# Row maxima of attention scores from a difference: positive part on ScalarE, sum and maximum on VectorE, scores in three PSUM banks

## The reference

```
q, k = _rope(q), _rope(k)
sim = jnp.einsum('bhid,bhjd->bhij', q, k) * SCALE
attn = jax.nn.softmax(sim, axis=-1)
out = jnp.einsum('bhij,bhjd->bhid', attn, v)
out = out.transpose(0, 2, 1, 3).reshape(b, n, HEADS * DIM_HEAD)
return out @ Wout + bout
```

## Time and profile before

| | us |
|---|---|
| median of 3 runs (1556.73 to 1557.29) | 1557.01 |
| time of the profiled execution | 1557.27 |
| its span, first to last instruction | 1555.5 |
| PE / PEld busy | 1424.9 / 546.8 |
| DVE busy, of it the 512 reductions L603 | 1222.0, 623.9 |
| ACT busy, of it the 1024 exps L515 | 778.3, 547.8 |
| POOL busy, of it the sums L676 | 977.8, 616.5 |
| PE idle ahead of unit matmuls (L397) until DVE's maximum was done | 47.7 |

### The profile page before, as it was taken

One profiled execution on the slowest core, in us unless ns is written; L12 is line 12 of the kernel. 1 busy time (PEld: TensorE's weight loads), 2 busy tenths in 40 slices (PEclk: granted clock), 3 DMA queues, 4 the chain that ended last, 5 costly groups with the idle time before them and its releaser, 6 DMA issues.

```text
span 1555.5 us, 25971 instructions
## 1 busy us (share of the span) xinstructions
PE 1424.9 (92%) x7289; PEld 546.8 (35%) x7289; DVE 1222.0 (79%) x1297; ACT 778.3 (50%) x1512; POOL 977.8 (63%) x501
## 2 busy tenths in 40 slices
PE   3689999999999999999999999999999999998886
PEld 1224333333333333333333333333333333333323
DVE  7787888788788878878788888878887887888744
ACT  3244554545454545555455454545545554544464
POOL 4388766658475665838476574848566584757731
PEclk9799999999999999999999999999999999999999
DMA  5312131221303121120313122031312204031002
GB/s 158 73 26 60 25 76 26 50 54 26 83 14 75 34 57 38 44 65 14 75 34 74 22 54 54 14 79 30 75 21 54 54 20 89 14 75 33 3 15 68
DMA packets 70209, 76.00 MB, mean 49 GB/s; under 512 B 27204, under 2 KB 36936, under 8 KB 69928
## 3 DMA queue, kind: packets, MB, share of 16 engines
q1 hardware_dynamic: 68736, 74.69, 21.4%
q10 hardware_dynamic: 1448, 1.00, 0.3%
HBM read 22.56 MB, written 2.36 MB: 16 GB/s over the span
## 4 chain that ended last, share of the span: by engine, by line
PE 56%; DVE 13%; issue 13%; POOL 7%; DMA 5%; ACT 3%; SPq 2%; DVEq 0%; ACTq 0%; POOLq 0%
PE O L388 18%; PE S L376 10%; PE S L377 8%; PE M L397 8%; DVE MX L603 5%; PE TILE L312 5%; DVE SUM L613 4%; DMA QK<-STAGE 4%; POOL SA L676 3%; PE TILE L322 2%; POOL STAGE L663 2%; ACT PF L515 2%; SPq L708 1%; PE TILE L306 1%; PE TILE L330 1%
## 5 line engine op out<-in xcount | busy, mean ns | idle before, releaser
L676 POOL TENSOR_TENSOR SA<-PF 128x1024 f32<-128x1024 f32 x256 | 616.5, 2424 | 372.5 <-DVE SUM L610 279.9
L515 ACT ACTIVATE PF<-S 128x512 f32<-128x512 f32 x1024 | 547.8, 599 | 564.9 <-PE S L377 564.1
L603 DVE TENSOR_REDUCE MX<-M 128x1 f32<-128x1024 f32 x504 | 614.5, 1219 | 229.3 <-PE M L397 229.1
L388 PE MATMUL O<-PF,V 128*64 128x512 f32 x2048 | 497.4, 607 | 0.0
L376 PE MATMUL S<-QK 128*128 128x512 f16 x1024 | 393.1, 384 | 0.0
L377 PE MATMUL S<-QK 128*128 128x512 f16 x1024 | 390.1, 381 | 0.0
L397 PE MATMUL M<-QK 64*128 64x512 f16 x1008 | 221.9, 437 | 65.9 <-DVE MX L603 47.7
L613 DVE TENSOR_TENSOR SUM<-SUM,SA 128x1024 f32<-128x1024 f32 x128 | 248.3, 1939 | 3.6 <-POOL SA L676 3.4
L397 PEld LDWEIGHTS M<-QK 64*128 64x128 f16 x1008 | 72.6, 140 | 370.8 <-DVE MX L603 247.9
L388 PEld LDWEIGHTS O<-PF,V 128*64 128x64 f32 x2048 | 124.5, 136 | 206.4 <-issue 149.8
L376 PEld LDWEIGHTS S<-QK 128*128 128x128 f16 x1024 | 99.9, 98 | 165.3 <-issue 64.2
(11 more groups left out here) (96 smaller groups left out, 749.0 us busy)
## 6 DMA issues: line engine op xcount, KB each, us to landing
QK<-STAGE SPq DMA_DIRECT2D x128, 256.0 KB, 3.9
QK<-STAGE SPq DMA_DIRECT2D x128, 128.0 KB, 3.1
RB<-den SPq DMA_DIRECT2D x128, 128.0 KB, 3.0
X<-in_L_attn_queries SPq DMA_DIRECT2D x4, 512.0 KB, 12.8
RT<-DS SPq DMA_DIRECT2D x128, 2.0 KB, 1.7
out<-X SPq DMA_DIRECT2D x8, 256.0 KB, 2.3
WRAW<-in_L_attn_Wkv SPq DMA_DIRECT2D x1, 1024.0 KB, 8.7
ROPE<-in_rope SPq DMA_DIRECT2D x1, 1024.0 KB, 12.0
```

The source lines that it names most:

```text
L388: mm = e.matmul(O[DH * z:DH * z + DH, :], V[:, h, kt * DH:(kt + 1) * DH], PF[:, t % SLOTS, z * HALF:(z + 1) * HALF], start=(kt == 0), stop ...
L515: e.activation(PF[:, t % SLOTS, z * HALF:(z + 1) * HALF], S[:, t % 2, z * HALF:(z + 1) * HALF], ACT.Exp, scale=EXP_SCALE).then_inc(exped, 1)
L603: e.tensor_reduce(MX[:, place % 2, q:q + 1], bank, AX, ALU.max).then_inc(max_read, 1)
L676: e.tensor_tensor(SA[:, (t // 2) % 2, :], PF[:, t % SLOTS, :], PF[:, t % SLOTS + 1, :], ALU.add).then_inc(two_summed, 1)
```

## The change

Of a query row a unit now gives, in place of 1024 products, two times 512: its products with the differences of keys k and k+512 (in the new bank MD), and those with keys 512 and up (in one of two new banks MR). Since max(a, b) = b + max(a - b, 0), ScalarE writes the positive part of MD to LEFT in SBUF (`act_left`, Relu), and VectorE adds LEFT and MR and takes the maximum of the row in one `tensor_tensor_reduce`. POOL makes the differences of the high parts of the keys once per group (`pool_keys_less`), and `hand_over` copies them too, with six DMAs per head instead of four. K is projected before Q, and several tiles change their steps. The scores get three banks in turn, MD one, MR two, O and T one each. A score matmul waits for the exp that last read its bank. ACT's copy of O stands behind the exps of its step and no longer ahead of them. Three small weight buffers share space with SA.

```diff
-HAND = 4 * 16
+LOWEST = -3.0e38
+HAND = 6 * 16
-QK_TILES = [(w, c, t) for w in "qk" for c in range(2) for t in ("rot", "pass")]
+ORDER = "kq"
+QK_TILES = [(w, c, t) for w in ORDER for c in range(2) for t in ("rot", "pass")]
-QK_AT = (1, 3, 5, 7, 9, 11, 13, 15)
-V_AT = {8: (1, 0), 10: (1, 1), 22: (0, 0), 24: (0, 1)}
+QK_AT = (1, 3, 4, 7, 8, 10, 11, 13)
+KD_AT = 9
+V_AT = {14: (1, 0), 16: (1, 1), 22: (0, 0), 24: (0, 1)}
-NORM_AT = {16: 1, 26: 0}
+NORM_AT = {13: 1, 26: 0}
-DOWN_AT = (12, 14, 16, 18, 21, 23)
+DOWN_AT = (12, 18, 21, 22, 23, 24)
...
-        S = pb("S", [P, 2, N], F32)
-        M = pb("M", [P, N], F32)
+        S = pb("S", [P, 3, HALF], F32)
+        MD = pb("MD", [P, 512], F32)
+        MR = [pb(f"MR{n}", [P, 512], F32) for n in range(2)]
...
+        def bank_of(t, z):
+
+            return ((0, 1), (2, 0))[t % 2][z]
...
-                wait(e, exped, 2 * n + z - 3)
+                wait(e, exped, 2 * n - ((0, 2), (3, 1))[t % 2][z])
...
+        def pe_unit(e, u, place, q, side):
+
+            wait(e, left_over, u)
+            wait(e, max_read, u - 1)
+            e.matmul(MD[:, :], QHH[0:DH, place, q:N:KT], KD[:, place, :], start=True, stop=True)
+            e.matmul(MR[side][:, :], QHH[DH:P, place, q:N:KT], KMH[DH:P, place, 512:N],
+                     start=True, stop=True).then_inc(unit_made, 1)
...
+        def act_left(e, u, side):
+
+            e.wait_ge(unit_made, u + 1)
+            wait(e, max_read, u - 1)
+            e.activation(LEFT[:, side, :], MD[:, :], ACT.Relu).then_inc(left_over, 1)
...
-            if kt == 2 and (not it.first or h > 0):
-                act_copy_out(e, it.i * GH + h - 1, (h - 1) % GH)
+            more = not (it.last and t + LEAD >= STEPS)
+            if t % 2 == 0 and more:
+                act_left(e, it.step(t + LEAD), t % 2)
             for z in range(2):
...
+            if kt == 2 and (not it.first or h > 0):
+                act_copy_out(e, it.i * GH + h - 1, (h - 1) % GH)
             act_tiles(e, it, t)
+            if t % 2 == 1 and more:
+                act_left(e, it.step(t + LEAD), t % 2)
...
-            e.wait_ge(unit_made, u + 1)
-            e.tensor_reduce(MX[:, place % 2, q:q + 1], bank, AX, ALU.max).then_inc(max_read, 1)
+            e.wait_ge(left_over, u + 1)
+            e.sem_inc(max_begun, 1)
+            e.tensor_tensor_reduce(LEFT[:, side, :], MR[side][:, :], LEFT[:, side, :], 1.0, LOWEST, ALU.add, ALU.max,
+                                   MX[:, place % 2, q:q + 1]).then_inc(max_read, 1)
...
+        def pool_keys_less(e, g):
+
+            e.wait_ge(rot_hi, g * 4 + 2)
+            e.wait_ge(pass_hi, g * 4 + 2)
+            keys = HIGH["k"]
+            e.tensor_tensor(KDS[:, :, :], keys[:, :, 0:512], keys[:, :, 512:N], ALU.subtract).then_inc(keys_less, 4)
...
                 sp.dma_start(QK[top, h, 0:3:2, :], STAGE[rows, 1:3, t, :]).then_inc(handed[h], 16)
+                sp.dma_start(KD[top, h, :], KDS[rows, t, :]).then_inc(handed[h], 16)
...
             for u in range(LEAD):
-                wait(pe, max_read, u - 2)
-                pe_unit(pe, u, u // KT, u % KT, (M[:, :], S[:, 0, :], S[:, 1, :])[u % 3])
-            pe.wait_ge(max_read, LEAD)
+                pe_unit(pe, u, u // KT, u % KT, u % 2)
```

More of the change, by code:

```diff
@@ L374, in pe_scores @@
                 rows = slice(z * HALF, (z + 1) * HALF)
-                wait(e, exped, 2 * n + z - 3)
-                e.matmul(S[:, t % 2, rows], KHL[:, h, keys], QHH[:, h, rows], start=True, stop=False)
-                e.matmul(S[:, t % 2, rows], KMH[:, h, keys], QML[:, h, rows],
+                wait(e, exped, 2 * n - ((0, 2), (3, 1))[t % 2][z])
+                e.matmul(S[:, bank_of(t, z), :], KHL[:, h, keys], QHH[:, h, rows], start=True, stop=False)
+                e.matmul(S[:, bank_of(t, z), :], KMH[:, h, keys], QML[:, h, rows],
                          start=False, stop=True).then_inc(scored, 1)
@@ L391, in pe_values @@
             mm.then_inc(pv_done, 1)
-        def pe_unit(e, u, place, q, bank):
-            for c in range(2):
-                rows, keys = slice(DH * c, DH * c + DH), slice(c * 512, (c + 1) * 512)
-                mm = e.matmul(bank[:, keys], QHH[rows, place, q:N:KT], (KHL, KMH)[c][rows, place, keys],
-                              start=True, stop=True)
-            mm.then_inc(unit_made, 1)
+        def pe_unit(e, u, place, q, side):
[4 more added lines that the diff above has]
+                     start=True, stop=True).then_inc(unit_made, 1)
         def pe_next_unit(e, it, u):
@@ L405, in pe_next_unit @@
                 e.wait_ge(handed[place], HAND * (it.i + u // STEPS + 1))
-            e.wait_ge(max_read, it.step(u))
-            pe_unit(e, it.step(u), place, q, M[:, :])
+            pe_unit(e, it.step(u), place, q, u % 2)
         def pe_step(e, it, t):
@@ L596, in split_ff_weights, with dve_max @@
                                    ALU.subtract).then_inc(f_w_lo, 1)
[L598 to L600 removed]
+        def dve_max(e, u, head, place, q, side):
             if q == 0:
                 wait(e, max_found, head - 1)
[L603 removed]
+            e.wait_ge(left_over, u + 1)
+            e.sem_inc(max_begun, 1)
+            e.tensor_tensor_reduce(LEFT[:, side, :], MR[side][:, :], LEFT[:, side, :], 1.0, LOWEST, ALU.add, ALU.max,
+                                   MX[:, place % 2, q:q + 1]).then_inc(max_read, 1)
         def dve_sum(e, head, h, part):
@@ L685, in pool_step @@
                     rot_add(e, args, it.i + 1)
+            if t == KD_AT and not it.last:
+                pool_keys_less(e, it.i + 1)
             if t % 2 == 0 and (not it.first or t > 0):
@@ L807, in _ @@
                     rot_low(pool, args, 0)
+                    if args[0] == "k" and args[1] == 1:
+                        pool_keys_less(pool, 0)
             ln_rstd(pool, 1)
@@ L862, in _ @@
             act.wait_ge(b1_turned, 1)
-            act.activation(B1[:, :], M[:, 0:FF // P], ACT.Copy).then_inc(b1_copied, 1)
-            act_max(act, 0, 0)
+            act.activation(B1[:, :], MR[0][:, 0:FF // P], ACT.Copy).then_inc(b1_copied, 1)
+            for u in range(LEAD):
+                act_left(act, u, u % 2)
+                if u == KT + 1:
+                    act_max(act, 0, 0)
             def body(e, it):
```

45 lines of the change are left out of this document (25 added, 20 removed).

## The result

The changed kernel takes 1571.32 us (median of four runs, 1569.38 to 1572.88) against 1556.91 (1556.73 to 1557.29): a ratio of 1.0092, 95% interval 1.0074 to 1.0109. It is slower by 14 us, where the forecast was 20 us faster, and lies above the range. The profiled execution took 1572.87 us with a span of 1570.9.

What follows compares the result with a forecast made beforehand. TensorE (92% busy) sets the pace, late mainly for VectorE's maxima. Loop -14.4, first iterations -4.6 and -2.6, last -2, start +4.2: -19.4, say -20, from about 1557 to 1537 us; range 1528 to 1546.

Steps and rivals of the forecast that it cites:

- rival B: VectorE's fused sum and maximum costs 1.37 us, delaying low parts at steps 4 and 8: 1553 us, chance 0.15.
- D: Rival: VectorE itself binds, if GpSimd slows the fused instruction to 1.85 us per unit: 1610 us, chance 0.05.
- Rival A: Neighbour tiles at steps 10 and 11 cost nothing, so 1.8 us more go in 15 iterations: 1510 us, chance 0.12.
- step 11: Q rot tile, waiting for the bank until VectorE's low part of step 10's tile: 1.8 us, where 0.35 stood.
- Rival C: ScalarE's alternating positive part, exp and copy don't overlap, pitch 0.60 not 0.48 us: 1575 us, chance 0.15.
- Rival E: The change works, but small waits add 1.2 us per iteration more than counted: 1556 us, chance 0.08.
- step 28: PV matmuls wait for ScalarE's copy of O, now behind the exps: 0.7 us per iteration.
- step 4: Tile there waits 0.3 us for the low part of step 3's tile, plus 0.1 for the unit.
- out17: Output tile of step 17, behind the V tile of step 16: a new wait of 0.15 us.
- The loop's sum: Late starts removed against new ScalarE and tile-bank waits: -0.9 us per iteration, -14.4 for sixteen.
- First iterations -4.6 -2.6: Extra gains there: two hand-over waits of 2.9 us, not 0.6 (-4.6); MX waits 8.0, not 2.6 (-2.6).
- Last -2: Last iteration waits a little more than others for maxima, so it gains 2 us extra.

Runs made afterwards that it cites:

- e8: Changed kernel with the twelve units ahead of the loop in more banks: 1567.13 us, ratio 1.0069 to the kernel before.
- e5: Changed kernel with only ScalarE's fourteen middle iterations written out instead of a loop: 1551.10 us, ratio 0.9962 to the kernel before.
- e1: Changed kernel with the Q/K tiles of steps 11 and 13 moved to steps 12 and 15: 1565.46 us, ratio 1.0033 to the kernel before.
- e14: Changed kernel with the high part of a step's tile ahead of ScalarE's copy of O: 1550.18 us, ratio 0.9952 to the kernel before.
- e10: Changed kernel with ScalarE's positive part over 256 of 512 columns in the loop: 1566.91 us, ratio 1.0066 to the kernel before.
- e3: Changed kernel with the fourteen middle iterations written out in every engine: 1543.05 us, ratio 0.9899 to the kernel before.
- e2: Changed kernel with O copied between the two exponentials of its step: 1569.76 us, ratio 1.0066 to the kernel before.
- e15: Changed kernel with the copy of O back ahead of the step's exponentials: 1595.07 us, ratio 1.0240 to the kernel before.
- e4: Kernel before with its fourteen middle iterations written out in every engine: 1560.56 us, ratio 1.0018 to the kernel before.

## Why the prediction was wrong, step by step

The mechanisms of VectorE were right. The three waits for the maximum, the hand-over wait and the normalisation's are gone. The fused operation takes 0.69 + 0.08 us (forecast 0.85, rival B 1.37; B and D fall). Rival A falls by the 1.90 at step 11. Rival C, the one on the slower side, had ScalarE's instructions 0.60 apart and named 0.54 as the limit. A positive part and the exponential behind it do start 0.61 apart in most steps, but there the exponential waits for its scores: it starts 2.97 behind the PV, 0.12 behind the end of its matmul, as the forecast had it. Where it need not wait they are 0.49 apart, with ScalarE written out 0.53, and an exponential and the positive part behind it 0.48. So C is refuted although its time, 1575, came near. Rival E, small waits of 1.2 us an iteration more than counted, is what the quiet iterations show; its time, 1556, lacks the clock and the first and last iterations. First scores 61.19: forecast 61.0, although only 2 us of the delay come from the bank I blamed (e8).

The new waits that I had named were right one by one: step 11 1.90 (1.8), step 28 0.73 (0.7), step 4 0.32 (0.4 with its unit), out17 0.14 (0.15). The groups view of VectorE in the changed kernel:

```profile
L625 DVE CUSTOM_DVE_ANT_0 LEFT<-MR,LEFT 128x512 f32<-128x512 f32 x512 | 353.3, 690 | 481.8 <-ACT LEFT L517 477.1 <-issue 3.4
...
L625 DVE DVE_READ_ACCUMULATOR2_ANT MX<- 128x1 f32 x512 | 42.2, 82 | 0.0
```

What failed, of the 35.4 us between forecast (-20, rounded from -19.4) and profiled spans (+15.4):

- **The loop's sum, "-4.77 + 3.85 = -0.9": 19.4 us in the fourteen middle iterations, the clock's 3.3 among them.** I walked the 32 steps inside an iteration and not across its end. ScalarE's turn of 2.5 us had been hidden by its idle 2.82 us, and I filled that time with a positive part at each side of the turn. It made step 1 0.96 late where I had 0.16: 0.8 of the miss. Missing too were 0.32 at PV of step 4 (same cause as step 28, where I did see it) and 0.16 behind the V tile, while three of the other four bank waits are 0.07 and not 0.16. These make 1.0; a quiet iteration is 1.2 above the forecast, 16 us in fourteen, and 0.2 I can't place. e5 shows that step 1 is on time when ScalarE alone has no loop. The order on ScalarE is not part of this miss: its wait at step 11 was forecast at 1.8.
- **The clock.** Those 3.3 us, and one stretch of half clock more in the last iteration. The first has one of 3.4 us behind step 11, where the kernel before had one of about 7 us behind its hand-over wait. I had priced the wait of 1.8 us at 1.8. In the middle iterations of e1 and e14, where it is gone or shortened, there are no falls.
- **"First iterations -4.6 -2.6": about 6 us.** The earlier trace rows has one long hand-over wait, not two, so 2.3 were never there. The rest: transposes of steps 26 and 27 come 3.04 and 1.84 us late, where one was 1.14 late before, each for the low part of the tile ahead of it (e14 left them as they are), and step 11 with the clock behind it. In VectorE's queue the first of these low parts stands behind a sum that waited 4.78 us for GpSimd (the row below this list). GpSimd works there without a gap for some 46 us in both kernels (from 106.56 after, from 101.88 before). Counted from the first scores, TensorE ends the scores of step 26 5.6 us sooner than before, and GpSimd starts its sum only 0.5 sooner. So much of what the waits for maxima and hand-over gave back was lost again there. This is read from the traces; no run changed it by itself.
- **"Last -2": 7.5 us.** GpSimd works without a gap there for some 36 us from step 7 on, in both kernels, at the normalised rows that TensorE transposes, and so little could be won; a second stretch of half clock (1.7 us), the copy of O, and the tiles moved together came on top. This reading is of the traces only; no run changed the last iteration by itself.
- **The end, counted at 0: 1.34 us**, not traced.

```profile
135.93 2.05 DVE L636 TENSOR_TENSOR SUM<-SUM,SA 128x1024 f32<-128x1024 f32 x1 [4.78 <-POOL SA L706]
```

Of the remark on the Trainium skill's "ScalarE: Activation LUTs", Rules for kernel authors: the operation that this page warns of was not the main loss. Halving it (e10) bought 4 us; the order of the copy of O and the high part in the same queue was worth 21 (e14). No run has VectorE do it, so the page's advice itself stands untested. The rule of the Trainium skill ("VectorE: DVE Perf Modes", Two Vector instructions with no wait between them) that an operation with accumulator output counts as two instructions agrees with the trace: 0.69 and 0.08 us.

## What to carry to other kernels

When work moves to an engine with idle time, ask what that idle time was hiding: here the turn of the engine's own loop and a copy that had been free. Order the queue of the newly loaded engine by who waits for each result: what frees a buffer that TensorE wants goes ahead of what is wanted a step later. Sum up late starts as what may be won at most: take one away and PE arrives earlier at the next, as halving VectorE's work showed (1.6 us an iteration of the 3.5 counted). And price the first and the last iteration by themselves: GpSimd, which had idle time in the loop, had none there for 36 to 46 us on end.

## What the runs showed of the hardware that was not expected

- At the turn of its loop ScalarE stood for 2.48 us between its last instruction and its next, which made step 1 0.96 us late. Writing ScalarE's loop out gained 1.45 us an iteration, TensorE's 0.51.
- With values computed in registers ScalarE's exponentials started 0.12 us behind the end of their scores, with constants in the loop written out 0.04.
- Waits of 1.66 to 1.74 us on TensorE were followed in some middle iterations, not in all (two of fourteen in the changed kernel, four in e3, six in e2), by a granted clock of 0.50 for about 3.4 us, 1.6 to 1.8 us lost each time. No middle iteration of e14 (waits up to 0.8), e15 (up to 1.14) and e4 (up to 1.59) shows it.
- The fused sum and maximum of a PSUM and an SBUF operand over 512 elements takes as long as a plain add, 0.69 us, with 0.08 for the accumulator; over 256, 0.42.
